# A graph layer's item projection: the first block of items as one load, early item loads dealt to the two queues in order of use

## The chip, the cores and the metric

The kernel runs on one core of one Trainium2 chip. The metric is device time in microseconds for one execution. The kernel before took 1086.66 us, the median of three runs (1086.34 to 1087.0). Its profile comes from one execution that took 1086.57 us. The span of the profile, from the first to the last instruction, is 1084.8 us.

## The reference

```python
h = item_feat @ W_item.T + b_item          # 10000 x 128
b = x @ W_user.T + b_user                  # 10000 x 128
x = layernorm(x + relu(adj @ h + b))       # adj is 10000 x 10000, float32
```

All arrays are float32. The layer norm is over the 128 features, without scale or shift.

## The kernel before, in words

The large product is `adj @ h`. The users are taken in 19 groups of 512 and one last group of 272. For each group the kernel streams the transposed adjacency matrix through SBUF in tiles of 1 MB: 128 partitions, four chunks of 128 items each, 512 users wide. A ring of five slots holds the tiles (`ADJ_RING`). ScalarE rounds each tile to a high part (`split_hi`, L525) and VectorE takes the difference as a low part (`split_lo`, L722). TensorE then adds three products for each chunk into PSUM: high tile with high h (L463), high tile with low h (L464), and low tile with high h (L470).

Before all that stands the stage this case is about, the item projection. It makes h, 10,000 rows, from the item features. The items are taken in 20 blocks of 512 items, numbered 0 to 19. A block is four chunks of 128 items, 256 KB in all. `project_items(t)` (L437) multiplies the chunks of block t by the item weights (L446). Each chunk is one float32 matmul of 128x128, which the trace shows as two passes, so a block is eight passes. `add_item_bias(t)` on VectorE (L687) adds the bias and writes h in full precision, `split_h(t)` on ScalarE (L542) rounds it, and POOL (L648) takes the low part of the first nine blocks. Four PSUM buffers (`H_PS_RING`) stand between TensorE and VectorE.

TensorE's program begins with `warm_up` (L432 to L435), eight float32 matmuls of constants that need no load. Then it waits for the weights and the bias (`w_bias`, L487), projects all 20 blocks in order, and goes on to the first group's products. The last block also has a chunk of 16 leftover items, which VectorE copies into place (`copy_items_tail`, L698) and TensorE multiplies at L450.

The loads of items are listed in `ITEM_LOADS` as ranges of blocks: 0, 1, 2, 3, 4-5, 6-7, 8-9, 10-13, 14-17, 18-19. Loads 0 to 9 are numbered in that order. Two engines issue loads, SyncE (SP) and ScalarE (ACT), each on a DMA queue of its own: in the profile SP's queue is q1 and ACT's is q10. Which load goes where is written out by hand:

- ScalarE issues, ahead of all its other work, the first half of block 0 (L611, 128 KB, `FIRST_ITEMS`), and then the loads that `ACT_LOADS` names (L613): block 1, block 3, blocks 6-7.
- SyncE issues the weights (L404, 128 KB) and then the other item loads in order (`load_items`, L340): the second half of block 0 (128 KB), block 2, blocks 4-5, 8-9, 10-13. Load 8 (blocks 14-17) waits until four blocks are projected, load 9 (blocks 18-19) until six are. Between these two come the two halves of the first adjacency tile (`load_first_half`, L364), and after load 9 come the other adjacency tiles (`load_adj`, L358).

`item_load_places(n)` (L325) gives source and destination of a load. Its `skip` leaves out of load 0 what the half load has brought. On TensorE, `project_items(0)` waits for the half (`first_items_landed`, L439) and, after two chunks, for the other half (L445). In DRAM the item array is laid out load after load, each load as 128 rows (L886), so the length of a row, and of a packet, follows from the load: 1 KB for half a block, 2 KB for a block.

Of the kernel before, what the change touches and what calls it, by code (L numbers as in the profile page):

```python
# [26 lines left out]
P = 128  # L27
# [4 lines left out]
N_ITEM = 10000  # L32
# [11 lines left out]
PER_TILE = 4  # L44
# [20 lines left out]
GUESTS = (ADJ_RING - GUEST_FROM) * PER_TILE  # L65
ITEM_SLOTS = OWN_SLOTS + GUESTS
ITEM_LOADS = ((0, 1), (1, 2), (2, 3), (3, 4), (4, 6), (6, 8), (8, 10), (10, 14), (14, 18), (18, 20))
FIRST_ITEMS = (0, PER_TILE // 2 * P)
ACT_LOADS = (1, 3, 5)
ITEM_RANGES = [(max(a * PER_TILE * P, FIRST_ITEMS[1]), min(b * PER_TILE * P, N_ITEM)) for a, b in ITEM_LOADS]  # L70
HALVES_BEFORE = 9
HIGH_HALF_AFTER = (11, 13)
LOW_HALF_AFTER = (13, 15)
# [42 lines left out]
def later(g, n):  # L116

    return not isinstance(g, int) or g >= n
# [7 lines left out]
def width(g):  # L126

    return NARROW if narrow(g) else WIDE


def tiles(g):

    return NARROW_TILES if narrow(g) else TILES


def last(g):

    return tiles(g) - 1
# [13 lines left out]
def tile_of(ring, slot, g):  # L152

    u = width(g)
    if u == WIDE:
        return ring[:, slot]
    flat = ring[:, slot].rearrange("p c u -> p (c u)")
    return flat[:, 0:NARROW_PER_TILE * u].rearrange("p (c u) -> p c u", u=u)
# [19 lines left out]
def full_chunks(t):  # L178

    return PER_TILE if t < LAST else LAST_FULL  # L180


def chunk(g, t, c):

    n = NARROW_PER_TILE if narrow(g) else PER_TILE
    if t < last(g):
        return t * n + c
    return USER if c == AT_USER else t * n + c - AT_FULL


def parts(g, t):

    steps = steps_to(g, t)
    if t == last(g):
        return [(range(AT_USER, AT_FULL), steps - 1), (tile_places(g, t), steps)]
    if t == 0 and not later(g, 1):
        return [(range(*HALVES[0]), steps - 1), (range(*HALVES[1]), steps)]
    return [(tile_places(g, t), steps)]


def gnn_kernel(nc, adj_t, adj_tail, x_t, adj_narrow, tail_narrow, x_narrow, item_t, w_item_bias, w_user_t, b_user, out, out_last):
    with ExitStack() as ctx:  # L202
        def sb(name, shape, dt=F32):
            return ctx.enter_context(nc.sbuf_tensor(name, shape, dt))
# [4 lines left out]
        def sem(name):  # L209
            return ctx.enter_context(nc.semaphore(name))  # L210
# [13 lines left out]
        items = sb("items", [P, OWN_SLOTS, PER_TILE * P])  # L224
# [34 lines left out]
        item_landed = [sem(f"item_landed{i}") for i in range(len(ITEM_LOADS))]  # L259
# [1 line left out]
        tail_landed = sem("tail_landed")  # L261
        x_landed = sem("x_landed")
        w_bias_landed = sem("w_bias_landed")
        first_items_landed = sem("first_items_landed")
        w_user_landed = sem("w_user_landed")
        out_stored = sem("out_stored")
        ident_zeroed = sem("ident_zeroed")
# [41 lines left out]
        def item_tiles(t, cols):  # L309

            at = t % ITEM_SLOTS
            if at < OWN_SLOTS:
                return items[:, :, :].rearrange("p s n -> p (s n)")[:, at * PER_TILE * P:at * PER_TILE * P + cols]
            slot, at = divmod(at - OWN_SLOTS, PER_TILE)
            return adj[:, GUEST_FROM + slot].rearrange("p c u -> p (c u)")[:, at * WIDE:at * WIDE + cols]

        def item_load(t):

            return [a <= t < b for a, b in ITEM_LOADS].index(True)

        def item_rows(first, end):

            return item_t[P * first:P * end].rearrange("(p n) -> p n", p=P)

        def item_load_places(n):  # L325

            first, end = ITEM_RANGES[n]
            a = ITEM_LOADS[n][0]
            skip = first - a * PER_TILE * P
            return item_tiles(a, skip + end - first)[:, skip:], item_rows(first, end)  # L330

        block = ctx.enter_context(nc.Block())

# [1 line left out]
        def _(sp):  # L335
            def load_items(n):
                a, b = ITEM_LOADS[n]
                if b > ITEM_SLOTS:
                    sp.wait_ge(h_product, b - ITEM_SLOTS)
                sp.dma_start(*item_load_places(n)).then_inc(item_landed[n], 16)  # L340
# [20 lines left out]
            def load_first_half(half):  # L361
                a, b = HALVES[half]
                rows = adj_t[0, 0:P * PER_TILE * WIDE].rearrange("(p c u) -> p c u", p=P, u=WIDE)
                sp.dma_start(adj[:, 0, a:b, :], rows[:, a:b, :]).then_inc(adj_landed[0] if half else half_landed, 16)  # L364
# [40 lines left out]
            for n in range(len(ITEM_LOADS)):  # L405
                if n == HALVES_BEFORE:
                    load_first_half(0)
                    load_first_half(1)
                if n not in ACT_LOADS:
                    load_items(n)  # L410
# [19 lines left out]
        @block.tensor  # L430
        def _(pe):
            def warm_up():  # L432
                ones = nc.const_aps.tensor(1.0, [P, P], F32)
                for b in range(WARM):
                    nc.tensor.matmul(z_ps[:, b % BLOCKS, :], ones, ones, start=True, stop=True)  # L435

            def project_items(t):  # L437

                pe.wait_ge(item_landed[item_load(t)] if t else first_items_landed, 16)  # L439
                if t >= H_PS_RING:  # L440
                    pe.wait_ge(h_full_made, t - H_PS_RING + 1)
                n = full_chunks(t)
                for c in range(n):
                    if t == 0 and c == PER_TILE // 2:
                        pe.wait_ge(item_landed[0], 16)  # L445
                    mm = nc.tensor.matmul(h_ps[t % H_PS_RING][:, c, :], item_tiles(t, PER_TILE * P)[:, c * P:c * P + P],  # L446
                                          w_item[:, :], start=True, stop=True)
                if t == LAST:
                    pe.wait_ge(items_tail_made, 1)
                    mm = nc.tensor.matmul(h_ps[t % H_PS_RING][:, n, :], items_tail[:, :], w_item[:, :],  # L450
                                          start=True, stop=True)
                mm.then_inc(h_product, 1)

            def tile_product(g, t, parity):
                s = t % PART_RING
                u = width(g)
                into = acc[parity][:, 0:u]
                high, low = tile_of(adj_hi, s, g), tile_of(adj_lo, s, g)
                for places, steps in parts(g, t):
                    pe.wait_ge(hi_made, steps)  # L460
                    for c in places:
                        k = chunk(g, t, c)
                        nc.tensor.matmul(into, h_hi[:, k, :], high[:, c, :], start=(k == 0), stop=False)  # L463
                        nc.tensor.matmul(into, h_lo[:, k, :], high[:, c, :], start=False, stop=False)  # L464
                    pe.wait_ge(lo_made, steps)
                    if t == last(g) and AT_USER in places:
                        nc.tensor.matmul(into, h_pack[:, :], tail_pack[:, 0:u], start=False, stop=False)  # L467
                    for c in places:
                        k = chunk(g, t, c)
                        mm = nc.tensor.matmul(into, h_hi[:, k, :], low[:, c, :], start=False, stop=(k == FULL - 1))  # L470
                mm.then_inc(tile_done, 1)

            def turn_back():

                for p, bs in enumerate(PIECE_BLOCKS):
                    pe.wait_ge(piece_done, p + 1)
                    for b in bs:
                        nc.tensor.transpose(last_ps[b], z_t[:, b * P:b * P + P], ident[:, :]).then_inc(block_turned, 1)  # L478

            def group(g, parity):  # L480
                if later(g, 2):
                    pe.wait_ge(z_added, g - 1)
                for t in range(tiles(g)):
                    tile_product(g, t, parity)

            warm_up()
            pe.wait_ge(w_bias_landed, 16)  # L487
            for t in range(TILES):
                project_items(t)
            for t in range(TILES):  # L490
                if t == LAST:
                    pe.wait_ge(w_lo_made, 1)
                    pe.wait_ge(h_pack_made, 1)
                if t < POOL_LOWS:
                    pe.wait_ge(h_lo_made, t + 1)
                else:
                    pe.wait_ge(h_lo_made_dve, t + 1 - POOL_LOWS)
                tile_product(0, t, 0)
            pe.wait_ge(pads_ready, 1)
            group(1, 1)  # L500
            with pe.Fori(1, LOOP_PAIRS + 1) as i:
                group(2 * i, 0)
                group(2 * i + 1, 1)
            group(GROUPS - 2, 0)
            group(GROUPS - 1, 1)
            turn_back()

        @block.scalar
        def _(act):
# [98 lines left out]
                    if t == at.spread_rstd:  # L608
                        spread_rstd(g - 1)

            act.dma_start(item_tiles(0, FIRST_ITEMS[1]), item_rows(*FIRST_ITEMS)).then_inc(first_items_landed, 16)  # L611
            for n in ACT_LOADS:
                act.dma_start(*item_load_places(n)).then_inc(item_landed[n], 16)  # L613
            for t in range(EARLY_BLOCKS):
# [286 lines left out]
```

## Time and profile before

| | before |
|---|---|
| median of three runs | 1086.66 us |
| the profiled execution | 1086.57 us |
| its span | 1084.8 us |
| TensorE (PE) busy | 1077.5 us, 99% |
| VectorE (DVE) busy | 962.0 us, 89% |
| ScalarE (ACT) busy | 835.5 us, 77% |
| POOL busy | 116.0 us, 11% |
| DMA | 417.14 MB, mean 385 GB/s |

The profile lists each engine's busy time. "PE" is the matmul side of TensorE, "PEld" its loading of weights. "SPq" and "ACTq" are the instructions with which SyncE and ScalarE issue loads. A timeline row gives the start, the length, the engine and line, the output and input, and in brackets how long the engine had been idle before and what ended the wait. The chain that ended last is followed back from the last instruction, each time to what released it. "To landing" is the time from the start of a load's issue until its completion is signalled.

### The profile page before, as it was taken

How to read it: one execution, taken by the hardware profiler on the slowest of the kernel's cores; microseconds unless marked ns; L12 is line 12 of the kernel's file. 1: busy time of each engine (PE TensorE's matmuls, PEld its weight loads, DVE VectorE, ACT ScalarE, POOL GpSimd, SP SyncE). 2: the span in 40 equal slices, each digit the busy share in tenths (PEclk: the TensorE clock that was granted, in tenths of full speed). 3: DMA queues.
4: the chain of work that ended last, by engine and by line, in shares of the span. 5: the costliest groups of instructions: out<-in, count | busy, mean ns of one | idle time of the engine just before them, and what ended most of it. 6: DMA issues, size and time to landing. Idle time of an engine off the chain costs nothing.

```text
span 1084.8 us, 14880 instructions
## 1 busy us (share of the span) xinstructions
PE 1077.5 (99%) x4937; PEld 900.4 (83%) x4937; DVE 962.0 (89%) x614; ACT 835.5 (77%) x801; POOL 116.0 (11%) x56
## 2 busy tenths in 40 slices
PE   9999999999999999999999999999999999999998
PEld 8888888888888888888888888888888888888888
DVE  6999898989898989898989898989898989898986
ACT  6878777878787878787778787878787878787875
POOL 4360000000000000000000000000000000000001
PEclk9999999999999999999999999999999999999999
DMA  9999999999999999999999999999999999999993
GB/s 369 417 376 421 348 423 353 423 354 424 367 423 366 424 364 423 361 423 370 424 363 422 353 423 364 422 356 422 365 421 353 422 361 422 359 423 361 421 354 142
DMA packets 66408, 417.14 MB, mean 385 GB/s; under 512 B 8194, under 2 KB 9284, under 8 KB 20052
## 3 DMA queue, kind: packets, MB, share of 16 engines
q1 hardware_dynamic: 65668, 415.63, 96.0%
q10 hardware_dynamic: 720, 1.25, 0.3%
q8 instruction: 13, 0.21, 0.1%
q14 instruction: 7, 0.06, 0.0%
HBM read 411.72 MB, written 5.12 MB: 384 GB/s over the span
## 4 chain that ended last, share of the span: by engine, by line
PE 99%; DMA 1%; DVE 0%; SPq 0%; issue 0%; DVEq 0%
PE acc L464 32%; PE acc L470 32%; PE acc L463 32%; PE h_ps L446 1%; DMA items<-item_t 1%; PE acc L467 0%; SPq L340 0%; DVE stats L789 0%; PE h_ps L450 0%; DVE items L812 0%; SPq L404 0%; DVE items L805 0%; PE z_ps L478 0%; DVE moments L796 0%; DVEq L202 0%
## 5 line engine op out<-in xcount | busy, mean ns | idle before, releaser
L722 DVE TENSOR_TENSOR adj_lo<-adj,adj_hi 128x2048 fp32r<-128x2048 f32 (+2 forms) x391 | 864.8, 2229 | 105.3 <-ACT adj_hi L525 104.4
L525 ACT CAST adj_hi<-adj 128x2048 fp32r<-128x2048 f32 (+2 forms) x391 | 724.1, 1864 | 146.8 <-DMA adj<-adj_t 92.0
L464 PE MATMUL acc<-adj_hi,h_lo 128*128 128x512 f32 (+1 forms) x1580 | 604.3, 384 | 0.0
L463 PE MATMUL acc<-adj_hi,h_hi 128*128 128x512 f32 (+1 forms) x1580 | 604.3, 384 | 0.0
L470 PE MATMUL acc<-adj_lo,h_hi 128*128 128x512 f32 (+1 forms) x1580 | 417.2, 384 | 0.0
L464 PEld LDWEIGHTS acc<-adj_hi,h_lo 128*128 128x128 f32 x1580 | 296.7, 188 | 58.4
L463 PEld LDWEIGHTS acc<-adj_hi,h_hi 128*128 128x128 f32 x1580 | 296.7, 188 | 58.4
L470 PEld LDWEIGHTS acc<-adj_lo,h_hi 128*128 128x128 f32 x1580 | 292.6, 188 | 58.4
L665 POOL TENSOR_TENSOR items<-items,minus_mean 128x512 f32<-128x512 f32 x19 | 39.1, 2058 | 586.7 <-ACT minus_mean L558 586.7
L669 POOL TENSOR_TENSOR items<-items,rstd_all 128x512 f32<-128x512 f32 x19 | 37.6, 1980 | 340.4 <-ACT rstd_all L579 340.4
L550 ACT COPY gathered<-part 32x16 f32<-32x16 f32 x152 | 30.8, 203 | 19.8 <-DVE part L760 10.4
L571 ACT ACTIVATE std<-total,eps 32x16 f32<-32x16 f32 x19 | 5.8, 307 | 44.4 <-DVE total L777 44.4
L653 POOL TENSOR_TENSOR h_pack<-h_tail,h_pack 17x128 fp32r<-17x128 f32 x1 | 26.5, 26482 | 26.7 <-ACT h_hi L542 26.7
L579 ACT COPY rstd_all<-rstd 32x16 f32<-32x16 f32 x76 | 15.4, 203 | 14.4 <-DVE rstd L784 13.7
L687 DVE TENSOR_TENSOR h_full<-h_ps,w_bias 128x512 f32<-128x512 f32 (+1 forms) x20 | 13.3, 674 | 8.2 <-PE h_ps L446 8.1
L558 ACT ACTIVATE minus_mean<-total 32x16 f32<-32x16 f32 x76 | 16.3, 214 | 5.2 <-DVE total L771 3.9
L542 ACT CAST h_hi<-h_full 128x512 fp32r<-128x512 f32 (+1 forms) x20 | 12.0, 607 | 7.4 <-DVE h_full L687 7.4
L717 DVE TENSOR_TENSOR tail_pack<-tail_in,tail_pack 16x512 fp32r<-16x512 f32 (+1 forms) x20 | 13.5, 676 | 0.6
L719 DVE TENSOR_TENSOR adj_lo<-xg,adj_hi 128x512 fp32r<-128x512 f32 (+1 forms) x20 | 13.8, 688 | 0.3
L754 DVE STREAM_TRANSPOSE items<-items 128x512 f32<-128x512 f32 x19 | 13.4, 704 | 0.0
L446 PE MATMUL h_ps<-w_bias,items 128*128 128x128 f32 x92 | 11.2, 278 | 1.8 <-DMA items<-item_t 1.8
L738 DVE SCALAR_TENSOR_TENSOR items<-acc,xg 128x512 f32<-128x512 f32 x19 | 13.0, 683 | 0.0
(51 smaller groups left out, 153.6 us busy)
## 6 DMA issues: line engine op xcount, KB each, us to landing
adj<-adj_t SPq DMA_DIRECT2D x360, 1024.0 KB, 7.7
adj<-adj_t SPq DMA_DIRECT2D x21, 512.0 KB, 5.3
adj<-adj_narrow SPq DMA_DIRECT2D x11, 952.0 KB, 7.4
xg<-x_t SPq DMA_DIRECT2D x19, 256.0 KB, 8.0
out<-items SPq DMA_DIRECT2D x19, 256.0 KB, 2.2
tail_in<-adj_tail SPq DMA_DIRECT2D x57, 32.0 KB, 4.4
adj<-item_t SPq DMA_DIRECT2D x1, 1024.0 KB, 10.9
items<-item_t SPq DMA_DIRECT2D x1, 1024.0 KB, 6.8
```

The lines of the kernel that those rows point to most:

```text
L446: mm = nc.tensor.matmul(h_ps[t % H_PS_RING][:, c, :], item_tiles(t, PER_TILE * P)[:, c * P:c * P + P], w_item[:, :], start=True, stop=True)
L463: nc.tensor.matmul(into, h_hi[:, k, :], high[:, c, :], start=(k == 0), stop=False)
L464: nc.tensor.matmul(into, h_lo[:, k, :], high[:, c, :], start=False, stop=False)
L470: mm = nc.tensor.matmul(into, h_hi[:, k, :], low[:, c, :], start=False, stop=(k == FULL - 1))
L525: nc.scalar.copy(into[:, places[0]:places[-1] + 1, :], source[:, places[0]:places[-1] + 1, :]).then_inc(hi_made, 1)
L550: ins = nc.scalar.copy(gathered[:, q, :], part[q * SQ:q * SQ + SQ, :])
L558: ins = nc.scalar.mul(minus_mean[q * SQ:q * SQ + SQ, :], total[:, :], -1.0 / HID)
L579: ins = nc.scalar.copy(rstd_all[q * SQ:q * SQ + SQ, :], rstd_32[:, :])
L653: nc.gpsimd.tensor_tensor(h_pack[again, :], h_tail[again, :], h_pack[again, :].bitcast(F32), ALU.subtract).then_inc(h_pack_made, 1)
L665: nc.gpsimd.tensor_tensor(centred, z_b, minus_mean[:, :, None].to_broadcast([P, BANDS, SQ]), ALU.add).then_inc(centred_made, 1)
L669: nc.gpsimd.tensor_tensor(z_b, centred, rstd_all[:, :, None].to_broadcast([P, BANDS, SQ]), ALU.mult).then_inc(out_ready, 1)
L722: nc.vector.tensor_tensor(into[:, places[0]:places[-1] + 1, :], source[:, places[0]:places[-1] + 1, :], high[:, places[0]:places[-1] + 1, ...
```

## The change

The load of the first half of block 0, its semaphore and the second wait inside block 0 go away. Load 0 now brings the whole of block 0 (256 KB) in one DMA. ScalarE issues loads 0, 2 and 4 (blocks 0, 2, 4-5), and SyncE the others (blocks 1, 3, 6-7, 8-9, ...). The order in which TensorE uses the blocks stays. The host's layout of the item array follows the new load ranges.

```diff
-FIRST_ITEMS = (0, PER_TILE // 2 * P)
-ACT_LOADS = (1, 3, 5)
-ITEM_RANGES = [(max(a * PER_TILE * P, FIRST_ITEMS[1]), min(b * PER_TILE * P, N_ITEM)) for a, b in ITEM_LOADS]
+ACT_LOADS = (0, 2, 4)
+ITEM_RANGES = [(a * PER_TILE * P, min(b * PER_TILE * P, N_ITEM)) for a, b in ITEM_LOADS]
...
-        first_items_landed = sem("first_items_landed")
...
             first, end = ITEM_RANGES[n]
-            a = ITEM_LOADS[n][0]
-            skip = first - a * PER_TILE * P
-            return item_tiles(a, skip + end - first)[:, skip:], item_rows(first, end)
+            return item_tiles(ITEM_LOADS[n][0], end - first), item_rows(first, end)
...
-                pe.wait_ge(item_landed[item_load(t)] if t else first_items_landed, 16)
+                pe.wait_ge(item_landed[item_load(t)], 16)
...
-                    if t == 0 and c == PER_TILE // 2:
-                        pe.wait_ge(item_landed[0], 16)
...
-            act.dma_start(item_tiles(0, FIRST_ITEMS[1]), item_rows(*FIRST_ITEMS)).then_inc(first_items_landed, 16)
             for n in ACT_LOADS:
                 act.dma_start(*item_load_places(n)).then_inc(item_landed[n], 16)
...
-        "item_t": np.concatenate([items[:, a:b].ravel() for a, b in [FIRST_ITEMS, *ITEM_RANGES]]),
+        "item_t": np.concatenate([items[:, a:b].ravel() for a, b in ITEM_RANGES]),
```

## Rows read from the trace of the kernel before

**Rows 1.** The page's busy times, and TensorE's granted clock in 40 slices.
```profile
PE 1077.5 (99%) x4937; PEld 900.4 (83%) x4937; DVE 962.0 (89%) x614; ACT 835.5 (77%) x801; POOL 116.0 (11%) x56
...
PEclk9999999999999999999999999999999999999999
```

**Rows 2.** Waits of TensorE's matmuls over the whole run: total us, times, longest.
```profile
PE h_ps L446 <- DMA items<-item_t: 1.8, 2, 1.5
```

**Rows 3.** Timeline of TensorE's matmuls from the start to 11.8 us.
```profile
0.78 3.38 PE L435 MATMUL z_ps<-const-float32-1.0 128*128 128x128 f32 x16 [0.78 <-PEq L892]
4.00 2.03 PE L446 MATMUL h_ps<-w_bias,items 128*128 128x128 f32 x16
7.51 2.05 PE L446 MATMUL h_ps<-w_bias,items 128*128 128x128 f32 x16 [1.48 <-DMA items<-item_t]
9.91 2.05 PE L446 MATMUL h_ps<-w_bias,items 128*128 128x128 f32 x16 [0.35 <-DMA items<-item_t]
```

**Rows 4.** The chain that ended last, its beginning: start us, us, what.
```profile
1.65 0.43 SPq L340
...
2.12 7.74 DMA items<-item_t
...
9.91 14.11 PE h_ps L446 x124
```

**Rows 5.** Timeline of the two issuing queues in the first 2.6 us.
```profile
0.74 0.40 SPq L404 DMA_DIRECT2D w_bias<-w_item_bias  x1
0.74 0.42 ACTq L611 DMA_DIRECT2D items<-item_t  x1
...
1.19 0.93 ACTq L613 DMA_DIRECT2D items<-item_t  x2
...
2.15 0.45 ACTq L613 DMA_DIRECT2D adj<-item_t  x1
```

**Rows 6.** DMA issues, 0 to 12 us (KB, us to landing); last row: L613, min/median/max.
```profile
items<-item_t SPq DMA_DIRECT2D x1, 512.0 KB, 7.7
adj<-item_t ACTq DMA_DIRECT2D x1, 512.0 KB, 8.4
adj<-item_t SPq DMA_DIRECT2D x1, 512.0 KB, 8.9
...
items<-item_t SPq DMA_DIRECT2D x1, 256.0 KB, 5.8
w_bias<-w_item_bias SPq DMA_DIRECT2D x1, 128.0 KB, 2.7
items<-item_t ACTq DMA_DIRECT2D x1, 128.0 KB, 2.9
items<-item_t SPq DMA_DIRECT2D x1, 128.0 KB, 3.2
...
DMA to landing us min/median/max: 3.6/6.3/8.4
```

**Rows 7.** DMA queues, 0 to 4 us: packets, MB, share; then one 2 us window.
```profile
q1 hardware_dynamic: 300, 0.29, 27.6%
q10 hardware_dynamic: 269, 0.36, 25.6%
...
4.00:6.00 2.00, 2.00 (x18) 1.84 (x16) 0.69 (x1) 0.04 (x1) 0.00 (x0) 1.00 0.96 276
```

**Rows 8.** Behind the projection: timelines at 24 to 29 us, and L364's landings.
```profile
23.82 0.18 DVE L698 COPY items_tail<-items 128x48 f32<-128x48 f32 x1
24.05 0.30 PEld L450 LDWEIGHTS h_ps<-w_bias,items_tail 128*128 128x128 f32 x2 [0.22 <-DVE items_tail L698]
25.64 2.28 DVE L722 TENSOR_TENSOR adj_lo<-adj,adj_hi 128x2048 fp32r<-128x2048 f32 x1
...
28.94 1.07 PE L470 MATMUL acc<-adj_lo,h_hi 128*128 128x512 f32 x4
...
DMA to landing us min/median/max: 7.7/8.1/8.5
```

## The prediction

> **What bounds the kernel now.** I read the busy times first. TensorE is busy 99% of the span and no other engine is above 89% [rows 1], so only TensorE's own idle time or extra work can move the end. I asked next what TensorE waits for. For loads it waits twice in the whole run, both times at L446 for items, 1.8 us together [rows 2]. The timeline of its matmuls places these waits. Warm-up ends at 4.16. Blocks 0 and 1 run from 4.00 without a pause (the passes overlap, so their times do too). Then there are 1.48 us of idleness until 7.51, blocks 2 and 3, another 0.35 us until 9.91, and from there no pause [rows 3]. The chain that ended last agrees. It goes from a SyncE issue at L340, begun at 2.12, through a DMA of 7.74 us that lands at 9.86, to L446 at 9.91, and from there it stays on TensorE [rows 4]. That load is blocks 4-5. So the start of the kernel is bounded by one landing, that of blocks 4-5, and just before it by that of block 2.
>
> This already caps the gain. If both waits vanished, 1.48 + 0.35 = 1.83 us would go, 0.17% of 1086.57. About 0.2% (2.17 us) is what a measurement of this kernel can tell from no change.
>
> **When each load lands before.** I add "to landing" to the start of the issue [rows 4 to 6]. Beside it I write the load's position, the KB that its own queue has been given up to and with it.
> On SP: weights 128 KB, 0.74 + 2.7 = 3.44. Second half of block 0, position 256, 1.19 + 3.2 = 4.39. Block 2, position 512, 1.65 + 5.8 = 7.45. Blocks 4-5, position 1024, 9.86. Blocks 8-9, position 1536, issued at about 2.60, 11.5.
> On ACT: first half of block 0, position 128, 0.74 + 2.9 = 3.64. Block 1, position 384, 1.19 + 3.6 = 4.79. Block 3, position 640, 1.65 + 6.3 = 7.95 (the middle of the three landings of L613; the second issue starts at about 1.65). Blocks 6-7, position 1152, 2.15 + 8.4 = 10.55.
>
> **The change, part by part.**
> 1. Block 0 becomes one load of 256 KB at the head of ACT, position 256. Its landing is bounded below by the old half, 3.64, and above by block 1's at position 384, 4.79. I take 4.3, next to the 4.39 of the old second half, which stood at the same position on the other queue. TensorE, free at about 4.0, starts some 0.3 us later (0 to 0.8). That costs nothing at the end: blocks 0 and 1 take 2.03 us [rows 3], so they end at about 6.4, or 6.9 at the bound, and block 2 cannot start before its load at about 7.4. The cover is the 1.48 us wait. If it were gone, the full 0.3 would be paid. One semaphore wait inside block 0 also goes, at nothing, in the same shadow.
> 2. Block 1 moves from ACT to SP, at the same position 384 and the same issue time. It is wanted one block after the start, at about 5.3, and 4.79 is early enough.
> 3. Block 2 moves from SP (position 512, issued at 1.65) to ACT (position 512, issued at 1.19). ACT's nearest rows are 4.79 at position 384 and 7.95 at 640, with 6.4 halfway between them. The bounds are therefore 6.4 and 7.95. I take 7.35, near the row of the same position, 7.45.
> 4. Block 3 moves to SP, position 640, between 7.45 at 512 and 9.86 at 1024, by proportion 8.05. It is wanted one block after block 2, at about 8.3. No wait of its own.
> 5. Blocks 4-5, the load that counts, move from SP (fourth issue, 2.12) to ACT (third issue, about 1.65), still at position 1024. ACT's rows on either side are 7.95 at 640 and 10.55 at 1152, by proportion 9.9. The row of the same position on SP says 9.86. Bounds: not after 10.55, which ACT needed for 128 KB more, and not before 9.1, which takes off 9.86 the 0.47 us of earlier issue and the upper end of the packet saving in point 6.
> 6. One DMA and 128 packets fewer lie ahead of everything. Packets in the first 4 us cost 0.276 x 16 x 4.0 / 300 = 59 ns on SP's queue and 61 ns on ACT's [rows 7]. Block 0 was 256 rows of 1 KB, 16 on each of the 16 engines, 0.94 us. Now it is 8 rows of 2 KB on each, which cost 8 x 59 = 0.47 us if the length were free and 0.94 us if twice the length costs twice the time. The saving is 0 to 0.47 us. As the DMA engines are 96% busy between 4 and 6 us and move only 276 GB/s there, with rows of 2 KB and more, I take it near the low end, 0.15 us.
> 7. ScalarE issues three loads instead of four, 0.45 us less [rows 5]. Its first casts come only after TensorE and VectorE have made block 0, so this hides. SyncE issues as many loads as before, its first waiting one included: load 8 still waits for block 3's product, and moves with it.
>
> The earlier issue in point 5 is worth nothing to me. Blocks 2 and 4-5 were issued 0.47 us apart and landed 2.4 us apart, and the DMA engines are at 96% of their time [rows 7]: the load stands in a queue of bytes, not behind its issue. The Trainium skill, page "DMA: Bandwidth & Descriptors", section "Issuing engines are not separate DMA queues", says that loads from all queues interleave on the same 16 engines and that a second issuing engine saves only the issuing time. Taken at its word, the 0.47 us of earlier issue would be the gain, and the sum would be -0.47 us instead of mine; the trace bears out the interleaving but not that issuing time was what lacked.
>
> So blocks 4-5 land at 9.86 - 0.15 = 9.71, and block 4 starts at about 9.75 instead of 9.91. Blocks 2 and 3 must be through by then: 7.35 + 0.06 + 2.05 = 9.46, so they are. **The sum is -0.16 us.**
>
> Is the gain kept behind it? Blocks 6-7 at SP position 1152 land at about 10.3 (between 9.86 and 11.5), wanted two blocks after 9.75, at 11.6. The adjacency halves landed at 17.7 and 18.9 [rows 8], issues at 9.96 and 10.40, and move with block 3's product. The tightest place is L450, whose weights waited 0.22 us for VectorE's copy at 23.82 [rows 8]. VectorE runs there at TensorE's pace and moves along, so I cost it at nothing; if it did not move, the gain would be lost. The next margin is tile 1: its low part is ready at 25.64 + 2.28 = 27.92 and wanted at 28.94, 1.0 us to spare [rows 8]. Nothing else of the kernel changes. 1086.57 - 0.16 = 1086.41 for an execution like the profiled one, which lay 0.09 under the median: 1086.5.
>
> **The rivals.**
> A. Nothing but a shift of some tenths, as above: 1086.1 to 1086.8. Chance 0.62. The case that the reordering does nothing at all, as the positions of blocks 2 and 4-5 do not change, lies in it: 1086.7.
> B. ACT's queue is the slower one. For it: blocks 6-7 at position 1152 landed at 10.55 where SP had 1024 at 9.86. If blocks 4-5 land on ACT as late as that, block 4 starts at 10.6 instead of 9.91, +0.7 us: 1087.3. Against it: by proportion both queues have position 1024 at 9.9. Chance 0.17.
> C. Both landings come clearly earlier, as blocks 2 and 4-5 are now second and third on a queue of three. If blocks 4-5 land at the bound of 9.1 and block 2 at 6.4, block 4 starts at 9.15 and 0.76 us go: 1085.9. The cap of 1.83 us gives 1084.8. Chance 0.16. Against it: the bytes ahead of them are the same.
> D. Slower: TensorE's clock. Warm-up takes 3.38 us for 16 passes, 0.21 each, against 0.127 for the item passes from 4.00 on [rows 3], although the granted clock is at its full level, 2.4 GHz, in every slice [rows 1]. The passes are slow until the warm-up's end. Today the items follow without a pause. With the whole of block 0 landing after 4.16 there is one. If TensorE then went on at 0.21, each pass would cost 0.085 us more, and the two waits would absorb the first 1.83 us. It decides from (2.17 + 1.83) / 0.085 = 47 slow passes, that is up to block 5; with ten blocks slow it is 80 x 0.085 - 1.83 = +5.0 us, 1091.6. Against it: the pause of 1.48 us at 6.03 left the passes after it at 2.05 / 16 = 0.128 us. Chance 0.03. The Trainium skill, "TensorE: Matmul & The Clock Gate", "Part 1: The HAM clock gate", holds that the clock starts throttled and that activity releases it, which speaks against any pause put in here; the trace agrees on the slow start and shows no fall after a pause.
>
> **How the numbers follow.** The predicted time is A's, 1086.5. The remaining 0.02 is for what I have not seen. The range 1085.5 to 1087.4 holds A and B whole and the nearer half of C, with the runs' own spread of 0.3 us to either side. Only D and the unseen reach beyond 0.2% on the slow side: 0.04. On the fast side the cap of 1.83 us lies inside 0.2%, so only the unseen and the spread on top of the full cap can do it: 0.03. Within 0.2%: 0.93.
>
> **What would show it.** In the profile after, TensorE's first item pass should start between 4.1 and 4.6, with a short pause behind warm-up and passes of 0.127 us. The wait before block 2 should shrink to about 1.0 us, because TensorE comes later, and the wait before block 4 should end between 9.6 and 9.9 on a load of L613 in place of L340. From there TensorE should show no wait before the end of the run. I am wrong if blocks 4-5 land before 9.1 or after 10.6, if block 3 or blocks 6-7 show a wait of their own, if L450 eats the gain, or if any pass of blocks 0 to 3 takes 0.2 us.

## The result and the profile after

The changed kernel takes 1085.36 us (median of 22 runs, 1084.76 to 1085.99). The kernel before takes 1086.66 us (22 runs, 1086.18 to 1087.25). The ratio is 0.9987, 95% interval 0.9981 to 0.9993. So 1.30 us are gone, 0.12%. The interval leaves out 1, so the gain is measured. It lies within the 0.2% that I had called "no change", but 0.14 us below the end of my range. I had forecast 0.16 us.

The timeline of TensorE's matmuls in the changed kernel, to be held against [rows 3]:

```profile
0.78 3.75 PE L431 MATMUL z_ps<-const-float32-1.0 128*128 128x128 f32 x16 [0.78 <-PEq L885]
4.33 6.68 PE L440 MATMUL h_ps<-w_bias,items 128*128 128x128 f32 x48
10.85 7.31 PE L440 MATMUL h_ps<-w_bias,adj 128*128 128x128 f32 x64
```

Both waits are gone. Blocks 0 to 5, 48 passes, run in one piece from 4.33, where before there were three pieces with 1.48 and 0.35 us between them. The next stretch, from block 6 on, starts at 10.85. In the profile before it started at 11.80 and it has the same length. The difference, 0.95 us, is nearly that of the two profiled executions, 0.91 us (1085.66 against 1086.57). So all of the gain is made ahead of block 6.

The landings, from the DMA issues between 0 and 12 us (KB, median us to landing), and, last, the shortest, middle and longest of ACT's three loads at L606. They answer to [rows 6]:

```profile
adj<-item_t SPq DMA_DIRECT2D x2, 512.0 KB, 7.0
...
items<-item_t ACTq DMA_DIRECT2D x2, 256.0 KB, 3.7
items<-item_t SPq DMA_DIRECT2D x2, 256.0 KB, 4.5
items<-item_t ACTq DMA_DIRECT2D x1, 512.0 KB, 5.9
...
DMA to landing us min/median/max: 3.3/4.1/5.9
```

Block 0 is signalled at 0.74 + 3.3 = 4.04, block 2 at 1.19 + 4.1 = 5.29, and blocks 4-5 at 1.65 + 5.9 = 7.55. Before, block 2 came at 7.45 and blocks 4-5 at 9.86. They come over 2 us earlier. The bytes given to their queue up to and with them are the same as before, so the stream as a whole must run otherwise. Two views show it. First windows of 2 us; the last three columns are granted clock, DMA share and GB/s. One window of the kernel before (the one ahead of it is in [rows 7]):

```profile
6.00:8.00 2.00, 0.52 (x5) 1.00 0.99 373
```

and three of the changed kernel:

```profile
2.00:4.00 2.00, 2.00 (x11) 1.00 0.83 294
4.00:6.00 2.00, 2.00 (x11) 1.00 1.06 410
6.00:8.00 2.00, 2.00 (x17) 1.00 1.03 416
```

Then the DMA packets between 4 and 6 us, of the kernel before:

```profile
DMA packets 263, 0.55 MB, mean 276 GB/s; under 512 B 25, under 2 KB 25, under 8 KB 263
```

and of the changed kernel:

```profile
DMA packets 370, 0.82 MB, mean 410 GB/s; under 512 B 34, under 2 KB 34, under 8 KB 370
```

The packets are about equally long, 2.1 and 2.2 KB. In the kernel before one took 2.0 x 16 x 0.96 / 263 = 117 ns, in the changed one 2.0 x 16 x 1.06 / 370 = 92 ns. I had read the share of 0.96 at 276 GB/s [rows 7] as "the engines are full". They were occupied, but they moved less in that time than they do in the changed kernel.

The means of 117 and 92 ns hide how uneven this is. The trace also keeps every packet by itself. Of the 263 packets that start between 4 and 6 us in the kernel before, 16 took over 0.3 us each, the longest 1.28 us, and 8.4 us together. The other 247 took 90 ns on average, and the 370 of the changed kernel 92 ns, none of them over 0.28 us. So the slump is a few packets that stall, and not a stream in which all packets are slower.

A load has landed when the last of its 16 completion signals has come. The trace has their times (us):

| | block 2: first, median, last | blocks 4-5: first, median, last |
|---|---|---|
| kernel before | 5.16, 5.70, 7.46 | 7.62, 8.55, 9.87 |
| changed kernel | 4.88, 5.24, 5.31 | 6.85, 7.38, 7.61 |

Before, the last signal of blocks 4-5 came 2.25 us after the first one, now it comes 0.76 us after it. The rate alone explains only a part of the earlier landing: between 4 and 8 us the changed kernel moves (410 - 276) x 2 + (416 - 373) x 2 = 354 KB more, which is 0.9 us at 414 GB/s. The median signal of blocks 4-5 comes 1.2 us earlier and the last one 2.3 us. So about half of the earlier landing is that the last signals no longer trail. That the trailing signals are those of the stalled packets is likely, but not shown, since the trace does not say which of the 16 engines a packet ran on.

What bounds the start now is in the chain that ended last (start us, us, what):

```profile
0.78 3.75 PE z_ps L431 x16
4.54 13.64 PE h_ps L440 x112
...
18.89 1.15 DVE adj_lo L723
...
22.96 0.11 DVE items_tail L691
...
23.12 0.49 PE h_ps L444 x2
```

No DMA is left in it. It runs over the warm-up and the item passes, and then over VectorE's work at 18 to 23 us. [rows 8] had shown TensorE's weights waiting 0.22 us for the last piece of it.

### The profile page after: what moved, and what is told of

It is laid out like the page before. It is cut to its first block, busy times and chain, and to the rows that moved or that the text cites. A ratio compares the mean times of both kernels' runs of the same rounds, so it can differ in the third digit from the quotient of the medians.

```text
span 1083.9 us, 14879 instructions
## 1 busy us (share of the span) xinstructions
PE 1078.4 (99%) x4937; PEld 901.7 (83%) x4937; DVE 963.1 (89%) x614; ACT 836.6 (77%) x801; POOL 116.2 (11%) x56
## 4 chain that ended last, share of the span: by engine, by line
PE 99%; DVE 1%; issue 0%; DVEq 0%
PE acc L458 32%; PE acc L464 32%; PE acc L457 32%; PE h_ps L440 1%; PE acc L461 0%; PE z_ps L431 0%; DVE adj_lo L723 0%; DVE h_full L680 0%; DVE stats L782 0%; PE h_ps L444 0%; DVE items L805 0%; DVE items L798 0%; PE z_ps L472 0%; DVE moments L789 0%; DVEq L201 0%
## 5 line engine op out<-in xcount | busy, mean ns | idle before, releaser
L753 DVE TENSOR_REDUCE part<-items 128x16 f32<-128x512 f32 x19 | 12.8, 676 | 0.0
```

## The experiments

Two questions: which part of the change makes the stream faster, and what bounds the start once it is. Each time stands beside runs of the kernel before on the same chip, so times from different chips are compared by their distance to these. "Slump" is the stretch between 4 and 6 us in which the kernel before moves 276 GB/s and the changed kernel 410. A profile is of one execution.

**A second profile of the kernel before.**

> The kernel before, unchanged, for a second profile of it. If the late landings of the first profile belong to the kernel, block 2 lands again at about 7.4 us and blocks 4-5 at about 9.9 us, the DMA engines move under 300 GB/s between 4 and 6 us, and TensorE waits about 1.8 us for items. If they were an accident of that one execution, blocks 4-5 land anywhere down to 7.6 us, as in the profile after the change, and the time is still about 1086.7 us.

It took 1086.24 us in its one timed run. TensorE's timeline:

```profile
0.78 3.76 PE L435 MATMUL z_ps<-const-float32-1.0 128*128 128x128 f32 x16 [0.78 <-PEq L892]
4.33 4.77 PE L446 MATMUL h_ps<-w_bias,items 128*128 128x128 f32 x32
9.59 2.05 PE L446 MATMUL h_ps<-w_bias,items 128*128 128x128 f32 x16 [0.49 <-DMA items<-item_t]
```

Block 2 landed at 6.95, blocks 4-5 at 9.53, at 303 GB/s between 4 and 6 us, just above the 300 that I had named. The slump belongs to the kernel. The waits do not all, against what I had expected: 0.49 us is left here of 1.8, because TensorE was later and block 2 landed 0.5 us earlier. Its passes were slow up to about 6.3 us, in an unchanged kernel (more below).

**The merge alone, and the order alone.**

```diff
-ACT_LOADS = (0, 2, 4)          # e1: the changed kernel with before's dealing
+ACT_LOADS = (0, 1, 3, 5)
```
```diff
-ACT_LOADS = (1, 3, 5)          # e2: the kernel before, halves kept
+ACT_LOADS = (2, 4)
```

> Only the merge: block 0 is one load of 256 KB on ACT, and ACT keeps blocks 1, 3 and 6-7, SP keeps 2, 4-5, 8-9. Theory M (the halved block 0, with its 1 KB rows and its extra DMA, slows the early stream): blocks 4-5 land at 7.6 to 8.2 us as after the change, DMA moves about 400 GB/s between 4 and 6 us, and the time is 1085.4 us, within 0.3 us of the changed kernel. Theory O (the dealing of the loads to the queues does it): blocks 4-5 land at 9.5 us or later and the time is 1086.4 to 1086.9 us.

> Only the order: block 0 still comes in two halves of 128 KB, the first on ACT and the second on SP, but blocks 2 and 4-5 are ACT's, blocks 1, 3, 6-7 are SP's. Theory M: the slump stays, blocks 4-5 land at 9.3 us or later, 1086.3 to 1086.9 us. Theory O: blocks 4-5 land before 8.2 us and the time is about 1085.4 us.

The merge alone takes 1085.57 us against 1086.42 (ratio 0.9992, 0.9983 to 1.0001), moves 418 GB/s between 4 and 6 us and lands blocks 4-5 at 1.65 + 5.6 = 7.25. Theory M holds in the stream and the time; the landing is even earlier than the 7.6 to 8.2 us that it had named. The interval of the ratio just takes in 1, but all 11 runs (1085.45 to 1085.79) lie below the lowest of the 27 runs of the kernel before (1085.85). The order alone takes 1088.68 us (1086.45 to 1089.65) against 1086.42, ratio 1.0018 (1.0009 to 1.0027): slower, which neither theory had said. It moves 331 GB/s between 4 and 6 us, so the slump stays, as theory M had it. Blocks 4-5, now behind fewer bytes on ACT, land at 7.85 all the same. That is what theory O had said and not theory M (9.3 or later): the dealing can bring a load forward even in the slump. But block 1 has become the third load on SP, behind the second half of block 0, and lands at 7.35. TensorE stands still after block 0:

```profile
4.33 1.91 PE L446 MATMUL h_ps<-w_bias,items 128*128 128x128 f32 x8
7.35 4.73 PE L446 MATMUL h_ps<-w_bias,items 128*128 128x128 f32 x40 [1.11 <-DMA items<-item_t]
```

So the new dealing is harmful with the halves, and no harm of it is seen with the whole block. Whether it adds something to the merge can't be told: the merge alone gives 0.85 us against its own runs of before, the whole change 1.30, and the intervals of the two ratios overlap. In e1's profile TensorE waited 0.16 us for block 0 and 0.24 us for block 3, in that of the changed kernel for neither.

**The length of the rows.**

```diff
+            if n == 0:             # e3: one DMA, 256 rows of 1 KB
+                return (items[:, 0, :].rearrange("p (h n) -> p h n", h=2),
+                        item_t[P * first:P * end].rearrange("(h p n) -> p h n", h=2, p=P))
```

> The changed kernel, but the one load of block 0 is made of 256 rows of 1 KB in place of 128 rows of 2 KB (the two halves of the block lie one behind the other in DRAM). Theory M by row length: the slump of the stream comes back, blocks 4-5 land over 1 us later than in the changed kernel (8.6 us or later) and the time goes up by 0.5 to 1.2 us, to 1085.9 to 1086.6 us. Theory M by the number of DMAs, and theory O as well: blocks 4-5 land within 0.4 us of 7.55 us and the time stays at 1085.4 us.

1085.74 us against 1086.42 (ratio 0.9995, 0.9986 to 1.0004), 391 GB/s, blocks 4-5 at 8.4 us. This is between the theories. Behind the rows of 1 KB, blocks 4-5 come 0.8 us later than in the changed kernel and block 3 at 1.65 + 6.4 = 8.05, for which TensorE waits 0.63 us, but the slump is not back. Two packets stall here, 0.91 and 0.92 us long, where the changed kernel has none, and block 3's 16 signals come over 2.2 us. It is one profile; that the rows of 1 KB made them stall is not shown.

**The number of loads in flight.**

```diff
-(6, 8), (8, 10), (10, 14)      # e4: ten DMAs ahead of the first wait, as before
+(6, 8), (8, 9), (9, 10), (10, 14)
```
```diff
+                elif n == 6:       # e6: the kernel before, SP's far loads held back
+                    sp.wait_ge(h_product, 1)
```

In e4 the loads are numbered anew by this, so `HALVES_BEFORE`, the number of the load ahead of which the first adjacency tile is loaded, goes from 9 to 10. In e6 the held loads were issued from 6.08 us on.

> The changed kernel, but blocks 8-9 come as two loads of 256 KB, so that ten DMAs are issued ahead of the first wait again, as before the change, with block 0 still whole. Theory N (what hurts the early stream is the number of DMAs in flight): the slump returns, under 340 GB/s between 4 and 6 us, blocks 4-5 land after 8.5 us, and the time is 1086 us or more. Theory H (it is the halved block 0 at the head of both queues): over 390 GB/s, blocks 4-5 land within 0.4 us of 7.55 us, and 1085.4 us.

> The kernel before, but SP holds the loads of blocks 8-9 and 10-13 back until block 0 is projected (about 5.3 us). Theory N, in its form that loads far down the queue take engine time from the near ones: blocks 4-5 land earlier than 9.9 us, by 0.5 us or more, and the time falls to about 1085.7 us. Theory H: block 2 still lands at 6.9 to 7.5 us and blocks 4-5 after 9.2 us; the time stays at 1086.4 us or rises, as the held loads come later.

Ten loads with block 0 whole: 1085.25 us against 1086.54 (0.9988, 0.9979 to 0.9997), 406 GB/s, blocks 4-5 at 7.55. The kernel before with fewer in flight: 1086.89 against 1086.54 (1.0001, 0.9992 to 1.001), 313 GB/s, block 2 at 7.65 and blocks 4-5 at 10.2. Theory N falls on both sides: a tenth DMA does not bring the slump, and holding two loads back does not end it.

**Where the halves lie, and what about them matters.** In e5 both halves are on ACT. In e12 the two loads split the partitions, so that their rows are 2 KB. In e13 block 0 is whole and block 1 comes in two loads with 1 KB rows.

```diff
-ACT_LOADS = (1, 3, 5)          # e5, from the kernel before
+ACT_LOADS = (0, 2, 4)
```
```diff
+            into, rows = item_load_places(0)      # e12
+            act.dma_start(into[0:64], rows[0:64]).then_inc(item_landed[0], 16)
+            act.dma_start(into[64:P], rows[64:P]).then_inc(item_landed[0], 16)
```
```diff
+                if n == 1:                        # e13
+                    for h in range(2):
+                        sp.dma_start(into[:, h * half:h * half + half],
+                                     item_rows(first + h * half, first + h * half + half)).then_inc(item_landed[n], 16)
```

> The changed kernel's order, but block 0 comes in two halves of 128 KB, both issued by ACT, one behind the other; SP's list is that of the changed kernel. Theory H: the stream slumps as before the change (about 300 GB/s between 4 and 6 us) and the time is 1086.3 us or more. Theory S (what hurts is the second half on SP's queue, ahead of the blocks there): no slump, blocks 4-5 (ACT, issued 0.45 us later than in the changed kernel) land by 8.3 us, and the time is 1085.3 to 1085.8 us. Theory N, ten DMAs ahead of the first wait: slump.

> The changed kernel, but block 0 comes as two loads of 128 KB that split the partitions (0 to 63, 64 to 127), with rows of 2 KB, both issued by ACT. Theory R (the slump needs 1 KB rows in two DMAs at the head): no slump, about 400 GB/s between 4 and 6 us, blocks 4-5 land by 8.2 us, 1085.2 to 1085.8 us. Theory D (two short DMAs at the head are enough, whatever their rows): slump as with the two halves on ACT, under 340 GB/s, blocks 4-5 after 9 us, over 1086.3 us.

> The changed kernel, but block 1, not block 0, comes in two loads of 128 KB with rows of 1 KB, both on SP. Theory R and theory D, if only the shape of the loads counts: slump, under 340 GB/s between 4 and 6 us, and over 1086.3 us. Theory F (it is what comes first, block 0, that must not be cut): no slump, about 400 GB/s, 1085.2 to 1085.8 us.

The window of 4 to 6 us of each (time, granted clock, DMA share, GB/s). e5, both halves on ACT, 1087.50 us against 1086.54 (1.0011, 1.0002 to 1.002), blocks 4-5 at 12.1 (the profiled execution, 1088.79 us, was a long one):

```profile
4.00:6.00 2.00, 1.00 0.92 251
```

e12, two loads with 2 KB rows, 1088.36 us against 1086.78 (1.0017, 1.0007 to 1.0026), blocks 4-5 at 11.1:

```profile
4.00:6.00 2.00, 1.00 0.98 289
```

e13, block 1 cut instead, 1085.75 us against 1086.78 (0.9993, 0.9983 to 1.0002), blocks 4-5 at 6.95:

```profile
4.00:6.00 2.00, 1.00 1.06 415
```

Theory S falls with e5, theory R with e12, theory F holds in e13. Not all of e12's lateness is the slump: ACT's two short issues took 0.56 and 0.60 us, block 2 was issued at 1.98 instead of 1.19 and block 0 was complete only at 5.47, for which TensorE waited 1.07 us.

In all the profiles, the stream slumps where ACT's first load is a half of block 0, whatever its rows and wherever the other half goes, and it does not where that load is the whole block. The packets say the same. Between 4 and 6 us, the eight profiles with a cut block 0 have 7 to 16 packets of over 0.3 us, the eight with the whole block none, but for the two of e3. The same cut one load later does no such harm.

Two things are not told apart here. Every kernel with a short first load on ACT also has the other half of block 0 as a second short load right behind it or beside it; no run has one without the other. And it is not any queue's first load: SyncE's first one, the weights, is 128 KB in all 16 profiles. Why the cut does this is not shown. The slump comes some 2 us after the stream has begun, and the profile does not say what the stalled packets wait for.

**What bounds the start now.** Twelve warm-up matmuls for eight, in both kernels, and seven in the changed one.

```diff
-WARM = 8
+WARM = 12                      # e7 after, e8 before; e9: 7, after
```

> The changed kernel with twelve warm-up matmuls in place of eight, eight passes more, at 0.21 us each with the clock low (1.7 us) or 0.12 with it high (0.9 us). Theory P (after the change the loads bind no longer, TensorE's own passes from 0.78 us on do): all of it comes on top, +0.9 to +1.7 us, 1086.3 to 1087.1 us. If a landing still bound the projection, as before the change, some of it would be hidden and the time would stay within 0.5 us of 1085.4 us.

> The kernel before with twelve warm-up matmuls in place of eight. Its two waits for loads, 1.83 us in the first profile, should take in the 0.9 to 1.7 us of further passes: within 0.3 us of 1086.5 us. If it goes up by over 0.8 us, the waits were not what bound the start.

> The changed kernel with seven warm-up matmuls, two passes fewer. Theory P: with warm-up over at 4.1 us in place of 4.5 us and block 0 landed at 4.04 us, TensorE starts its items some 0.2 to 0.4 us earlier, 1085.0 to 1085.2 us. If the clock comes later because less was done before, the gain is lost or turned round: 1085.4 us or more.

The changed kernel goes to 1086.31 us (0.9998, 0.9989 to 1.0007), 0.95 more than without; by the distances to the kernel before it is 1.30 - 0.23 = 1.07 more. The kernel before stays: 1086.78 against 1086.75 (0.9998, 0.9989 to 1.0007). Eight more passes are free where a landing binds, and cost about the 0.9 us of eight passes at the full clock where it doesn't. Theory P holds. With seven the time is 1085.55 us (0.9987, 0.9978 to 0.9996), no better than with eight and not the 1085.0 to 1085.2 that theory P had named. In the profile TensorE ends its warm-up sooner and then waits 0.30 us for block 0, which landed at 4.24, so it starts its items at 4.37 as against 4.33. Warm-up and first landing are level. A clock that comes later was the other way to lose the gain; this one profile does not show it (its 48 passes took 5.67 us).

**The clock.**

> The order alone (halves kept) once more, for a second look: its runs spread from 1086.45 to 1089.65 us, and its profile came from the fast end. Theory C (the pause behind block 0, 1.1 us in that profile, sometimes keeps TensorE's clock low for longer): a profile from the slow end shows passes of 0.2 us after the pause, up to 9 us or beyond. Theory L (the loads vary): passes of 0.12 us after the pause, and longer waits for items.

> The changed kernel once more, for a second look. Its 22 runs fall in two lots, about 1084.9 and about 1085.6 us, and its profile (1085.66 us) showed item passes at 0.21 us until about 6.3 us. Theory C: a run of the fast lot shows 0.12 us passes from about 4 us on, and no wait or a short one; one of the slow lot looks like the first profile.

e10 took 1089.4 us, near the longest of that kernel's earlier runs. Its timeline, and two of its windows (length, PE busy, granted clock, DMA share, GB/s):

```profile
4.33 1.10 PE L446 MATMUL h_ps<-w_bias,items 128*128 128x128 f32 x8
8.00 6.26 PE L446 MATMUL h_ps<-w_bias,items 128*128 128x128 f32 x40 [2.56 <-DMA items<-item_t]
```
```profile
6.00:8.00 2.00, 0.00 (x1) 0.96 1.03 398
8.00:10.00 2.00, 2.00 (x9) 0.50 1.04 427
```

Here the granted clock falls to 0.50, the lower of its two levels, 1.2 GHz, behind a pause of 2.56 us. 40 passes then take 6.26 us, where the first profile of this kernel had 4.73. Both the longer wait and the clock are in it, so theories C and L each have a share. It is one execution; that the clock makes the whole spread is not shown.

The length of the pause alone does not decide. In e5 TensorE stood still for longer, 3.04 us, and the granted clock stayed at 1.00:

```profile
9.56 2.05 PE L446 MATMUL h_ps<-w_bias,items 128*128 128x128 f32 x16 [3.04 <-DMA items<-item_t]
```

Its 16 passes behind the pause take 2.05 us, as without one.

e11, the changed kernel once more, took 1085.37 us, between the two lots that I had named:

```profile
4.33 6.14 PE L440 MATMUL h_ps<-w_bias,items 128*128 128x128 f32 x48
10.30 7.31 PE L440 MATMUL h_ps<-w_bias,adj 128*128 128x128 f32 x64
```

The same 48 passes took 6.68 us in the first profile after and 5.69 us in e4 (ten loads). No wait stands between them in any of the three; what differs is how many of the first passes take 0.21 us. Between 5 and 6 us, the first profile after has six passes of this sort (mean ns of one, pipelined):

```profile
L440 PE MATMUL h_ps<-w_bias,items 128*128 128x128 f32 x6 | 1.5, 421 | 0.0
```

while e1 had eight passes of mean 288 ns there:

```profile
L440 PE MATMUL h_ps<-w_bias,items 128*128 128x128 f32 x8 | 1.3, 288 | 0.1
```

It is not the change that does it: the second profile of the kernel before has the slow passes too, the first hasn't. TensorE's passes leave the slow rate at another moment in each execution, before 4.0 us in the first profile of before and after 6.0 us in the first profile after. The granted clock reads 1.00 in the windows of all of them, but for the first microseconds that is no reading. The trace's record of the clock has no entry there, and the view prints 1.00 for it. The first entry, at full level, stands at 3.62 us in the first profile of before and at 6.49 in the second, at 6.75 in the first profile after, 5.53 in e11 and 4.07 in e4. In each of these profiles the passes up to that entry are shown 421 ns long and start 0.21 us apart, and those behind it are shown 275 ns long, with starts 0.11 us apart. Starts 0.21 us apart are also what e10 has under the recorded 0.50. So the passes of the first microseconds ran at the lower level, 1.2 GHz, and the 48 passes took the longer the later the clock rose: 6.68, 6.14 and 5.69 us for 6.75, 5.53 and 4.07.

In the profiles of the kernel before, the waits for loads hid most of this scatter. Now it is seen. It may be what spreads the 22 runs into two lots, 11 up to 1085.21 us and 11 from 1085.50 us on, but only one of them has a profile, so that is not shown.

e4 shows what comes next when the passes are fast early, the loading of weights at L444 (L450 before):

```profile
22.29 0.30 PEld L444 LDWEIGHTS h_ps<-w_bias,items_tail 128*128 128x128 f32 x2 [0.44 <-DVE items_tail L691]
```

Block 6 started there at 9.82, 1.03 us ahead of the first profile after, and 0.44 us of idleness for VectorE's copy stand against it, as against 0.2 there.

## Why the prediction was wrong

- The size failed, not the place. That only TensorE's two waits could be gained, that they are worth 1.83 us at most, and that the landing of blocks 4-5 sets the end: all as forecast. The warm-up runs show it from both sides: eight more passes cost nothing before, with the landings binding, and about 1 us after. The measured 1.30 us are 0.7 of the cap.
- **The term that failed is point 6**, one load and 128 packets fewer, priced at 0.15 us between 0 and 0.47. I priced packets at their mean cost, as if the load were worth what its own packets take. The whole change moved the landing of blocks 4-5 by 2.3 us (9.86 to 7.55), and the merge alone by 2.6 us in its profile (to 7.25) and the time by 0.85 us. What it took away was the stalls behind it: 16 packets of 0.3 to 1.28 us between 4 and 6 us, and completion signals of blocks 4-5 that trailed by 2.25 us. Why the halved load brings them stays open.
- The bounds by queue position (points 3 and 5: block 2 not before 6.4, blocks 4-5 not before 9.1) failed with it: the landings were at 5.29 and 7.55. All their rows came from the slumped stream. A bound from rows that share the cost one is about to remove bounds nothing. The 9.1 was also added up wrongly: 9.86 less 0.47 and less the upper end of point 6, 0.47, is 8.92. And the 6.4 was no bound but the middle between two rows, of which the lower is 4.79.
- Point 1: block 0 landed at 4.04, not 4.3, and TensorE started at 4.33 as forecast, but for another reason: the warm-up was slower. The whole block had landed by then, so in this profile it costs TensorE nothing; in e1 and e9 TensorE waited 0.16 and 0.30 us for it. The cover that I had counted on, the wait for block 2, is gone.
- The dealing to the queues (points 2 to 5) I called neutral by the positions. Beside the merge it can't be told from neutral; without the merge it costs 2.26 us. There the position was half a guide: block 1 at position 512 on SP landed at 7.35, where block 2 had landed at 7.45 from the same place, but blocks 4-5 at position 896 on ACT landed at 7.85, where ACT's rows give 7.95 + 256 / 512 x 2.6 = 9.25 by proportion.
- Earlier issue, which I called worth nothing, was not tried alone. The Trainium skill, page "DMA: Bandwidth & Descriptors", section "Issuing engines are not separate DMA queues", lets a second issuing engine save the issuing time only, which I had put at 0.47 us; no run here shows it by itself. My argument for it, engines at 96% of their time, was the misread share.
- That the gain is kept behind it held in the first profile, where the 0.95 us come out as 0.91, with L450's successor (L444) as the next to bind, as said.
- Rival C was the case, beyond the part of it that my range took in: 1085.9 was its price for landings at the bounds, the cap's 1084.8 its end, and the result lies between. The argument that I set against it, the same bytes ahead, was the same error. Rival B fell. Rival D did not occur in the changed kernel, where items follow the warm-up without a pause, but its mechanism exists: e10 shows the clock falling behind a pause of 2.56 us, which the pauses of 1.48 us before and of 3.04 us in e5 did not bring. Its reading of the clock was wrong: the first slice is 27 us long, the record has nothing for its first 3.62 us, and the page prints the full level there. The slow warm-up passes were at 1.2 GHz.
- My sign "any pass of blocks 0 to 3 takes 0.2 us" came true and meant nothing about the change. One profile of the kernel before could not tell that its fast passes from 4.00 on were luck.

## What to carry to other kernels

A DMA share near 1 with fewer GB/s than elsewhere in the same trace need not be a full engine. Before calling the stream saturated, compare the time per packet with that of another stretch with packets of the same size, and look at the longest packets and not only at their mean. A load is as late as the last of its parts. Cutting the first load so that the first matmul can start sooner is a trade to be measured: here the half came 0.4 us earlier and block 1 some 0.3 us earlier, and the loads from block 2 on came 1.1 to 2.3 us later. And where a wait hides an engine's own scatter, one profile of the kernel before does not show what will be left when the wait goes.

## What the runs showed of the hardware

- A first load of 128 KB on ACT's queue, in place of one of 256 KB, leaves the stream at 251 to 341 GB/s between 4 and 6 us (eight profiles); with 256 KB it is 391 to 419 (eight profiles, one of them with block 1 cut instead, 415). In all of the former, the other half of block 0 comes as a second short load.
- In the same window, 7 to 16 packets took over 0.3 us with the cut block (up to 1.46 us, in e5), and none or two (e3, 0.92 us) with the whole one. The 16 signals of blocks 4-5 came over 1.2 to 3.2 us with it and over 0.3 to 1.1 us without.
- The granted clock fell to 0.50 behind a pause of 2.56 us, after TensorE had been busy from 0.78 to 5.4 us (e10). Behind a pause of 3.04 us, after it had been busy from 0.79 to 6.5 us, it stayed at 1.00 (e5).
- TensorE's passes left the slow rate of 0.21 us at moments up to 3 us apart, with the first entry of the clock record at 3.62 us in the first profile of before and at 6.75 in the first profile after. The warm-up of both is the same, and TensorE had been busy from 0.78 us on.
